# A fused attention and mixture-of-experts kernel: all four heads' probabilities turned through memory instead of three

## The reference

```python
x = x + xattn(layernorm(x), ctx, w_q, w_k, w_v, w_o, b_o)
#   q = x @ w_q, k = ctx @ w_k, v = ctx @ w_v        16 heads of 64
#   attn = softmax(q k^T / 8);  out = attn v;  out @ w_o + b_o
x = x + ffn(layernorm(x), router_w, router_b, w1, b1, w2, b2)
#   gates = softmax(x @ router_w + router_b), the best 2 of 8 experts,
#   each expert takes at most 640 tokens in token order;
#   y = sum over the chosen experts of gate * (gelu(x @ w1 + b1) @ w2 + b2)
```

## Time and profile before

| | us |
|---|---|
| median of 3 runs | 924.2 |
| profiled execution, whole | 930.95 |
| its span, first to last instruction | 929.2 |
| PE busy in the span | 897.7 (97%) |
| DVE busy | 719.8 (77%) |
| ACT busy | 539.7 (58%) |
| POOL busy | 398.6 (43%) |

### The profile page before, as it was taken

How to read it: one execution, slowest core, us unless ns; L and a number is a source line. 1 busy time by engine, 2 the same in 40 slices (tenths; PEclk the granted TensorE clock), 3 DMA queues, 4 the chain that set the end, 5 groups by cost and what they waited for, 6 DMA issues and landing times.

```text
span 929.2 us, 21961 instructions
## 1 busy us (share of the span) xinstructions
PE 897.7 (97%) x7692; PEld 796.4 (86%) x7692; DVE 719.8 (77%) x1603; ACT 539.7 (58%) x1544; POOL 398.6 (43%) x595
## 2 busy tenths in 40 slices
PE   8999999999999999999999999999898999999995
PEld 7888888888888888888888888887788999999995
DVE  5656778888897788888888888887876877668762
ACT  5787765666666576676567666666543443334420
POOL 5561425545464553636455463633343213332123
PEclk9999999999999999999999999999999999999998
DMA  8463777668777667766766777667138556554322
GB/s 238 142 205 107 224 209 223 199 202 224 228 213 232 212 188 216 235 200 217 233 184 198 220 224 205 204 186 231 58 117 167 98 136 147 123 121 73 105 30 29
DMA packets 152990, 162.61 MB, mean 175 GB/s; under 512 B 62141, under 2 KB 141611, under 8 KB 152753
## 3 DMA queue, kind: packets, MB, share of 16 engines
q1 hardware_dynamic: 127920, 130.21, 47.7%
q10 hardware_dynamic: 16128, 22.03, 8.6%
q0 software_dynamic: 8832, 8.98, 5.6%
HBM read 96.83 MB, written 69.29 MB: 179 GB/s over the span
## 4 chain that ended last, share of the span: by engine, by line
PE 62%; DVE 15%; ACT 7%; DMA 6%; issue 5%; SPq 2%; POOL 1%; another core or an unknown queue 0%; POOLq 0%; ACTq 0%; DVEq 0%
PE psum L793 18%; PE psum L1061 9%; PE psum L920 9%; PE psum L1045 8%; PE psum L904 8%; PE psum L860 6%; DMA squares<-prob 5%; ACT prob L1133 3%; PE psum L883 2%; DVE prob L1355 2%; DVE negmax L1326 2%; DVE hidl L1272 2%; DVE bufl L1272 1%; DVE ql L1315 1%; DVE attended L1346 1%
## 5 line engine op out<-in xcount | busy, mean ns | idle before, releaser
L1133 ACT ACTIVATE prob<-psum,negmax 128x256 f32<-128x256 f32 x512 | 240.5, 491 | 138.1 <-DVE negmax L1326 138.1
L1326 DVE TENSOR_REDUCE negmax<-psum 128x2 f32<-128x512 f32 x256 | 158.6, 682 | 30.8 <-PE psum L860 30.8
L663 POOL TENSOR_TENSOR al<-attended,ah 128x512 fp32r<-128x512 f32 x56 | 72.3, 1291 | 196.6 <-ACT ah L1072 196.5
L769 POOL DMA_INDIRECT out_rows<-y,rowi x40 | 66.3, 1658 | 161.6 <-DVE y L1583 155.0
L1244 ACT ACTIVATE hid<-psum,b1t 128x640 f32<-128x640 f32 x64 | 51.0, 796 | 126.9 <-PE psum L1045 126.9
L904 PE MATMUL psum<-probt,v 128*64 128x256 f32 x1024 | 124.6, 385 | 0.0
L1133 ACT ACTIVATION_READ_ACCUMULATOR prob<-psum,negmax 128x1 f32 x512 | 114.1, 223 | 0.0
L1355 DVE STREAM_TRANSPOSE prob<-prob 128x1024 f32<-128x1024 f32 x112 | 107.9, 964 | 0.0
L904 PEld LDWEIGHTS psum<-probt,v 128*64 128x64 f32 x1024 | 67.7, 136 | 38.4 <-issue 9.7
L1061 PE MATMUL psum<-w2h,hidh 128*128 128x256 f32 x320 | 91.4, 286 | 3.6 <-DVE y L1583 2.1
L726 POOL DMA_INDIRECT slot_table<-row,picki x64 | 67.3, 1051 | 61.9 <-PE psum L793 25.7
(11 more groups left out here) (208 smaller groups left out, 2625.5 us busy)
## 6 DMA issues: line engine op xcount, KB each, us to landing
squares<-prob SPq DMA_DIRECT2D x56, 768.0 KB, 5.8
probt<-squares SPq DMA_DIRECT2D x112, 192.0 KB, 4.1
probt<-squares ACTq DMA_DIRECT2D x112, 192.0 KB, 3.7
invrows<-inverses SPq DMA_DIRECT2D x128, 128.0 KB, 3.9
w1r<-in_w SPq DMA_DIRECT2D x8, 1024.0 KB
w2r<-in_w SPq DMA_DIRECT2D x8, 1024.0 KB
slot_table<-blank SPq DMA_DIRECT2D x8, 662.5 KB, 6.5
blocks<-slot_table SPq DMA_DIRECT2D x56, 80.0 KB
```

The costliest lines, as they stand in the source:

```text
L663: pool.tensor_tensor(al[:, b % 2, c:c + 2, :], attended[:, :, :], ah[:, b % 2, c:c + 2, :].bitcast(F32), ALU.subtract).then_inc(sem("a_lo" ...
L769: pool.indirect_dma_start(out=out_rows, out_offset=bass.IndirectOffsetOnAxis(ap=rowi[:, e % 2, s:s + 1], axis=0), in_=y[:, e % 2, s, :], i ...
L1133: last = act.activation(into, out_of, ACT.Exp, bias=negmax[:, m % 2, u, qb:qb + 1], accum_out=total[:, m % 2, u, qb:qb + 1])
L1326: dve.tensor_reduce(negmax[:, m % 2, u, :], psum[:, u, :].rearrange("p (q s) -> p q s", q=ST), AX.X, ALU.max, negate=True).then_inc(sem("m ...
```

## The change

`HEADS` goes; a function says how many heads of a period go through memory, and as `WHOLE` holds all four of a round's periods, it is 4 throughout. `MOVED` begins at period 4, two periods earlier. So in periods 4 to 61 there is no `turn3` and no `copy3`, `square1` takes two heads instead of one and waits for `exp3` instead of `exp2`, and each of the transfers of the probabilities is a third larger. ACT issues `move_high` ahead of `exp3` instead of behind it. SP's order becomes `move_low`, `inv_out`, `lift`, `inv_in`, `traffic`. `POOL_REST` begins one period earlier (the split `a_lo` of period 3 goes from VectorE to GpSimd).

```diff
-MOVED = range(6, PERIODS - 2)
-HEADS = 3
-POOL_REST = range(PER_B, PERIODS - 4)
+MOVED = range(4, PERIODS - 2)
+WHOLE = range(PER_B)
+POOL_REST = range(PER_B - 1, PERIODS - 4)
+def moved_heads(m):
+    return 0 if m not in MOVED else UNITS if m % PER_B in WHOLE else UNITS - 1
 def by_pe(m):
-    return (HEADS,) if m in MOVED else (0, 1, 2, 3)
+    return tuple(range(moved_heads(m), UNITS))
...
-            out += [("q", m + 1), ("k", m + 1), ("turn3", m - 1), ("pv", m - 2), ("v", m)]
+            out += [("q", m + 1), ("k", m + 1)] + ([("turn3", m - 1)] if by_pe(m - 1) else []) + [("pv", m - 2), ("v", m)]
...
-            out += [*steps("exp0 exp1", m), ("q_hi", m + 1), ("exp2", m), ("k_hi", m + 1), ("exp3", m),
-                    ("move_high", m - 1), ("copy3", m - 1), ("a_hi", m - 2), ("v_sb", m)]
+            out += [*steps("exp0 exp1", m), ("q_hi", m + 1), ("exp2", m), ("k_hi", m + 1), ("move_high", m - 1),
+                    ("exp3", m)] + ([("copy3", m - 1)] if by_pe(m - 1) else []) + [("a_hi", m - 2), ("v_sb", m)]
...
-        out += [("inv_out", m - 1)] + ([("move_low", m - 1)] if m - 1 in MOVED else [])
+        out += ([("move_low", m - 1)] if m - 1 in MOVED else []) + [("inv_out", m - 1)]
+        out += ([("lift", m)] if m in MOVED else []) + [("inv_in", m - 1)]
         out += [("traffic", b - 2)] if r == 1 and 2 <= b else []
-        out += [("inv_in", m - 1)] + ([("lift", m)] if m in MOVED else [])
...
-    out += [*steps("inv_out move_low inv_in", m - 1), ("load_w", 0), *steps("inv_out inv_in", m), ("inv_out", z),
+    out += [*steps("move_low inv_out inv_in", m - 1), ("load_w", 0), *steps("inv_out inv_in", m), ("inv_out", z),
...
-                heads = (slice(0, 2), slice(2, HEADS))[part]
+                heads = (slice(0, 2), slice(2, moved_heads(m)))[part]
                 dve.wait_ge(sem("exp"), UNITS * m + heads.stop)
```

More of the change, by code:

```diff
@@ L186, in timeline @@
     o0, o1 = ST * e, ST * e + 1
-    out += [("scores", m), ("q", z), ("k", z), ("turn3", m - 1), ("pv", m - 2), ("v", m),
+    last = by_pe(m - 1)
+    out += [("scores", m), ("q", z), ("k", z)] + ([("turn3", m - 1)] if last else [])
+    out += [("pv", m - 2), ("v", m),
             ("o", ST * d), ("x2t", c), ("scores", z), ("pv", m - 1), ("logits", c),
@@ L192, in timeline @@
             ("logits_part", o1), ("spread", 0), ("spread", 1), ("pos", e), ("base", 0), ("spread", 2), ("spread", 3)]
-    out += [*steps("exp0 exp1", m), ("q_hi", z), ("exp2", m), ("k_hi", z), ("exp3", m), ("move_high", m - 1), ("copy3", m - 1), ("a_hi", m - 2), ("v_sb", m), ("x2t_sb", c),
+    out += [*steps("exp0 exp1", m), ("q_hi", z), ("exp2", m), ("k_hi", z), ("exp3", m), ("move_high", m - 1)]
+    out += [("copy3", m - 1)] if last else []
+    out += [("a_hi", m - 2), ("v_sb", m), ("x2t_sb", c),
             *steps("exp0 exp1", z), ("w_hi", 0), ("a_hi", m - 1), ("copy0", m), *steps("exp2 exp3", z), ("w_hi", 1),
@@ L282, in build @@
         inv_table = nc.dram_tensor("inverses", [2, SQ, P], F32, kind="Internal").ap()
-        square_table = nc.dram_tensor("squares", [2, P, HEADS * ST * S], F32, kind="Internal").ap()
+        square_table = nc.dram_tensor("squares", [2, P, UNITS * ST * S], F32, kind="Internal").ap()
         table = nc.dram_tensor("slot_table", [NE * CAP, ROW], F32, kind="Internal").ap()
@@ L376, in prob_most, with square_rows_of @@
         def prob_most(m):
-            return flat(prob[:, m % 2, 0:HEADS, :, :, :])
+            return flat(prob[:, m % 2, 0:moved_heads(m), :, :, :])
         def probt_most(m):
-            return flat(probt[:, m % 2, 0:HEADS, :, :])
+            return flat(probt[:, m % 2, 0:moved_heads(m), :, :])
+        def square_rows_of(m):
+            return square_table[m % 2][:, 0:moved_heads(m) * ST * S]
         xn = turning[:, :].rearrange("p (t d) -> p t d", t=ST)
@@ L525, in lift @@
                     sp.wait_ge(sem("pv"), m - 1)
[L526 removed]
+                sp.dma_start(square_rows_of(m), prob_most(m)).then_inc(sem("lifted"), 16)
             def move_low(m):
@@ L660, in a_lo @@
                     pool.wait_ge(sem("a_lo"), m)
+                if m == PER_B:
                     pool.wait_ge(sem("table_clear"), 16 * NE)
@@ L898, in pv @@
                             cols = slice((2 * (c + cc) + h) * HD, (2 * (c + cc) + h + 1) * HD)
-                            if m in MOVED and 2 * cc + h < HEADS:
-                                p = probt_most(m).rearrange("p (a u k q i) -> p u k q a i", a=GROUPS, u=HEADS, k=ST,
+                            if 2 * cc + h < moved_heads(m):
+                                p = probt_most(m).rearrange("p (a u k q i) -> p u k q a i", a=GROUPS, u=moved_heads(m), k=ST,
                                                            q=ST)[:, 2 * cc + h, kb]
@@ L1126, in exps @@
                     into, out_of = prob[:, m % 2, u, :, qb, :], psum[:, u, qb * S:(qb + 1) * S]
-                    if m in MOVED and u < HEADS:
-                        into = prob_most(m).rearrange("p (g u k q j) -> p u q k g j", g=GROUPS, u=HEADS, k=ST,
+                    if u < moved_heads(m):
+                        into = prob_most(m).rearrange("p (g u k q j) -> p u q k g j", g=GROUPS, u=moved_heads(m), k=ST,
                                                      q=ST)[:, u, qb]
```

2 lines of the change are left out of this document (1 added, 1 removed).

## The result

The median went from 924.3 to 951.2 us (947.5 to 953.7), ratio 1.0292, 95% interval 1.0268 to 1.0315. The forecast of 918.7 us has the wrong sign and 951.2 lies outside its range of 903 to 938. The profiled execution took 947.5 us (span 945.7); 930.95 before. First scores of period 3 to those of period 63: 602.7 us before, 620.9 after, so all of the loss in these two traces is here; what follows took 285.9 and 285.2. The traces show only part of the loss in the medians: the profiled executions are 16.6 us apart (947.5 is the fastest of the four after, 930.95 above all four of before), the medians 27. What the other 10 us are, no trace shows.

A forecast was written before the change was run, and what follows sets the result against it. TensorE's work in order was taken as the bound. Terms -5.6 - 3.6 + 3.7 = -5.5 us took the profiled 930.95 us to 925.4, or the median of 924.2 to 918.7 us; range 903 to 938.

The forecast's parts named there:

- TensorE's saving: On TensorE, 64 heads' transposes go at 0.44 us each, 28.2 us, leaving 24 heads (96 matmuls).
- VectorE as the new bound: In the 13 rounds with a router, VectorE replaces TensorE as bound: gain 0.43 us each, 5.6 us in all.
- the logits' wait: Sign on TensorE: the router's logits wait for ScalarE's turned rows 1.3 to 1.8 us instead of 0.32, 13 times.
- the term of 39.57 us a round: VectorE's routed round: work 36.24, waits for ScalarE 2.31, about 0.45 more waiting, hand-over gaps 0.57 us.
- Volume does not bind; order may: DMA engines: larger transfers make 32 to 34 us busy of a 39.6 us round, so only their order might bind.
- point of decision: Landing time of the probabilities' write from which the write-and-read loop sets the period: 6.6 us; about 6 expected.
- the ring: Loop through ScalarE's DMA queue: write lands, reads, fourth head's exponentials, transpose, next write; landing + 3.3 us, 9.3 expected, hidden.
- rival 2: Slower: the ring through the queue decides, holding exponentials on ScalarE every period; some 935 us (+11), chance 0.33.
- Rival 1: VectorE hides its added work and only the logits chain pays: 908.7 us, at best 895; chance 0.15.
- Early periods: Periods 4 to 11, TensorE stays bound: 6.1 us gained, 2.5 lost to period 4's clash with slot-table clearing; gain 3.6.
- New order: Write ahead of sums and x, read started once the write has landed: helps its landing by some 1.2 us.
- End of the attention: After the last read, sums in and weights go out some 3.7 us later against TensorE: cost 3.7, bounds 0 and 5.

The follow-up runs named there:

- small: Kernel after the change, each transfer of squares (probabilities) carrying three quarters of its bytes, all four heads still transposed on VectorE: ratio 1.0095 to the kernel before.
- smallturn: Kernel after, transfers of squares at three quarters of their bytes and ScalarE's copy of the turned rows put first: 920.0 us, ratio 0.9949.
- turnfirst: Kernel after, ScalarE's copy of the turned rows put before the context's high part and v's copy: 946.8 us, ratio 1.0190.
- acto: Kernel after, ScalarE's two reads of squares put back behind head 3's exponentials, SyncE's order left as changed: ratio 1.0257.
- narrowturn: Kernel after, second transpose over one head instead of two, copy of the turned rows first, full transfers: mean period 10.3 us; total time not given.

## Why the prediction was wrong, step by step

**TensorE's saving** was right: 96 matmuls left, and a period that nothing else holds is 0.42 to 0.44 us shorter (8.24 for 8.66, 10.56 for 11.00).

**VectorE as the new bound** was the right place, and its signs came: DVE at 0.91 of the round shown (0.89 from 200 to 600), the 2.19 us wait gone, the logits' wait at 1.7 us. The step that failed is the term of 39.57 us a round; 41.4 were measured. Its base was short: a round before takes 40.2 us, not 40.0, which makes the sum 39.75 and leaves the saving of 0.43. The larger part is the chain into the logits. On TensorE's side the round shown adds up exactly: 40.18, less 1.67 us of work, plus 2.22 us more of idle time, is 40.73. Of the 2.54 us idle 1.71 are the logits and 0.63 the scores behind k's low part. The prediction had the logits' wait at 1.3 to 1.8 us, but put only 0.45 us for it into VectorE's sum, which left TensorE 39.57 - 38.24 = 1.33 us of waits in all, and it had none for the scores. On VectorE's side it is 36.88 us of work where a whole round by the same reckoning has 36.42 (34.25 + 2.17), and 3.85 us idle where I had 3.33. The layer norm's stretching adds 0.88 to the work and comes in front of the logits (last section).

The mean round is 0.64 us longer than the one shown. Three of twelve r0 periods last 14.4 to 14.6 us instead of 12.9, with the clock down: 4.6 us in all, 0.38 a round. The other 0.26 is in single r1 and r2 periods.

`small` tests the term without large transfers: 41.2 a round with the same VectorE work. So it is too small by itself, whatever the transfers do. That smallturn ran at 39.7, next to my figure, is partly luck: in that run the copy was moved and the logits don't wait, in the kernel that I forecast they do.

**"Volume does not bind; order may"** failed. I compared a sum of DMA time with the round and a median landing with a point of decision. The median stayed at 5.8 and hid a tail to 9.6, and with VectorE's work narrowed and the copy moved it was 7.2, over the ring's point of decision. Whether the longest landings cost anything in after itself, no run separates. The 436 GB/s that I reckoned with stand beside a DMA share of 1.11, more than the whole, so a rate over 2 us is too high: from 433 to 437 the same trace has 356 GB/s at 0.94. By ratio, shrinking the transfers is worth 18 us here (1.0292 to 1.0095; 5 in the traces) and 22 with turnfirst (1.0190 to 0.9949), narrowing VectorE 5 and nothing, and both together 46 (1.0292 to 0.9795).

**The rivals.** I set forecast and rival 2 against each other, 0.52 to 0.33, as if one of them would decide. Both act. In after the ring's own waits are small (11.5 + 6.0 us), since VectorE's are ahead of it; alone, each keeps the round at 41.2 to 41.4. Rival 1 is out in this kernel, as even with small transfers the round did not go under 39.7 while VectorE had the wide transposes. That taking head 3's exponentials out of the ring (acto) gained nothing does not speak against the ring: VectorE was the other limit in that run. How much a ring without those exponentials would bring with narrow transposes was not tried.

**Early periods**: forecast 3.6 us gained, 3.4 lost (89.2 to 92.6 from period 3 to 12), by period m6, 5.8 us longer where I had 2.5 for the clash, and by m10, 1.0 longer; the others gained as forecast. **New order**: right in kind, it helps, by far more than the 1.2 us of landing suggest (1.045 against 1.029). **End of the attention**: forecast 3.7 us lost and a wait of `a_norm` above 6 us; the wait was 1.38, but sums in did go out later and TensorE lost 2.4 us there. So the cost was right in kind, and the sign to watch for it was the wrong one.

## What to carry to other kernels

When a change loads two resources at once, work out the length of the loop through each and ask for both: if they are close, removing either alone shows little (5 and 18 us by ratio here, for 46 with both), and only a run without both tells what the change could bring. Judge a ring of transfers by its landings with the other limits taken away, the longest ones included, not by the median in the tuned kernel. When the bound is a chain, count the waits that it makes on the engine that it stops, not only the work in it. And look at what is copied behind the wait: 4.5 us lay in the place of one ScalarE copy, and a change may pay in the periods that have room for it, here two of four.

## Not expected of the hardware

**VectorE beside GpSimd.** The layer norm's apply, before and after, from 200 to 600: duration in ns min/median/max.

```profile
L1288 DVE TENSOR_SCALAR row<-x,ln_mean_var,ln_rstd x20: 404/408/417, 202.0 to 564.1; 128x256 f32<-128x256 f32 x20
```

```profile
L1301 DVE TENSOR_SCALAR row<-x,ln_mean_var,ln_rstd x20: 401/772/1292, 207.5 to 580.8; 128x256 f32<-128x256 f32 x20
```

The GpSimd instruction that it now meets:

```profile
414.94 1.28 POOL L676 TENSOR_TENSOR al<-attended,ah 128x512 fp32r<-128x512 f32 x1 [3.04 <-ACT ah L1085]
```

Before, this `al` ran at 400.54 to 401.83, mostly in VectorE's idle time. The `al` of r0 met the router's `gates` before (1655 ns in the mean, 221 after) and meets `chosen` now (211 ns before, 1087 after), so that stretching is only moved; the layer norm's is new. The Trainium skill, "SBUF — State Buffer", section "SBUF: two separate sides", says that the two engines share one pair of SBUF ports, and whichever of certain VectorE forms and a GpSimd instruction comes first holds it for its whole length. The rows agree in kind: up to 1.29 us against 0.40, with an `al` of 1.28 us beside it. They don't show that the first one holds: `gates` is recorded from 422.01, ahead of its `al` at 422.48, and yet ends with it (423.83 and 423.78). That the overlap is the cause is read from the rows and was not tested by itself.

**The clock.** In three of the twelve rounds TensorE's granted clock fell at the logits, at 1.5 us each. In the one of the second stretch above it had paused for 0.83 us before the scores and, after 1.7 us of mostly work, for 1.71 us before the logits; from 468 to 471 the clock was then 0.50, the lower level (1.2 GHz). A second had pauses of 0.98 and 1.70 us, the third a single one of 1.90. The other nine have pauses of 0.6 to 1.1 and of 1.7 us, and no dip. A pause of 4.8 us was followed by 0.50 too. In turnfirst and smallturn, without the 1.71, the clock is 1.00 (2.4 GHz) from 200 to 600; narrowturn doesn't have it either, and still one r0 period lasts 14.07 us at 0.50, after a pause of 1.12. What tips it is open.
